# Graph convolution kernel: four buffers of marks and taken rows in the first and third convolution, and 28 gathered groups of the first turned into 20 bucketed ones

## The reference

```python
src, dst, norm = _gcn_norm(edge_index, n)          # with self loops, norm = deg^-1/2[src] * deg^-1/2[dst]
def _gcn_conv(x, src, dst, norm, W, b, n_nodes):
    h = x @ W
    msg = h[src] * norm[:, None]
    out = jax.ops.segment_sum(msg, dst, num_segments=n_nodes)
    return out + b
h = jnp.maximum(_layernorm(x, axis=-1), 0.0)
x = x + _L0_gnn_ref(h, edge_weight, edge_attr_3, edge_index, ...)
h = jnp.maximum(_layernorm(x, axis=-1), 0.0)
for W, b in ((W1, b1), (W2, b2), (W3, b3)):
    h = jax.nn.relu(_gcn_conv(h, src, dst, norm, W, b, n))
return x + h
```

## Time and profile before

| | |
|---|---|
| median of 3 runs | 4809.85 us (4805.98 to 4815.88) |
| the profiled execution: time, span | 4815.22 us, 4813.4 us |
| PE busy | 3897.2 us, 81% |
| DVE busy | 3588.3 us, 75% |
| POOL busy | 3497.7 us, 73% |
| ACT busy | 2682.7 us, 56% |
| indirect DMAs (line 760) | 3552, mean 977 ns |

### The profile page before, as it was taken

The page is one execution under the profiler, slowest core; times in us unless marked ns, Lnnn a source line. Parts: engine busy times, 40 slices in busy tenths (PEclk is TensorE's granted clock), DMA queues, the critical chain, the costliest instruction groups (busy, mean ns, idle before and its releaser), DMA issues.

```text
span 4813.4 us, 182574 instructions
## 1 busy us (share of the span) xinstructions
PE 3897.2 (81%) x69021; PEld 2928.7 (61%) x69022; DVE 3588.3 (75%) x8527; ACT 2682.7 (56%) x6468; POOL 3497.7 (73%) x3596
## 2 busy tenths in 40 slices
PE   4988888888888888847666666898999999777776
PEld 2655555555555555535555555688888887556564
DVE  8999999999999999878777777544444444666666
ACT  4555555555555555468777777455555555544443
POOL 6777777777777777547777777477777776577775
PEclk9999999999999999956555555899999999776766
DMA  3111111111112112333333333443434444445544
GB/s 100 41 40 40 40 40 40 40 40 40 40 40 40 40 40 40 41 69 99 92 85 91 92 92 84 125 116 114 122 114 117 120 115 119 132 145 147 146 146 119
DMA packets 493903, 401.86 MB, mean 83 GB/s; under 512 B 266471, under 2 KB 454796, under 8 KB 492481
## 3 DMA queue, kind: packets, MB, share of 16 engines
q10 hardware_dynamic: 150164, 212.59, 13.1%
q0 software_dynamic: 113664, 104.82, 11.7%
q1 hardware_dynamic: 229360, 74.44, 7.1%
HBM read 376.21 MB, written 15.29 MB: 81 GB/s over the span
## 4 chain that ended last, share of the span: by engine, by line
POOL 68%; issue 23%; DVE 3%; PE 3%; ACT 1%; DMA 1%; POOLq 1%; DVEq 0%; ACTq 0%; SPq 0%
POOL rows L760 68%; PE radial L2168 1%; PE radial L2028 0%; DMA rows<-table,idx 0%; PE radial L2181 0%; ACT accT L926 0%; PE sums L1903 0%; DVE scratch L1098 0%; DMA xn<-in_x 0%; DMA scratch<-places_d 0%; DMA table<-arena 0%; PE radial L1969 0%; DVE rows L1788 0%; PE radial L1982 0%; PE psX L2046 0%
## 5 line engine op out<-in xcount | busy, mean ns | idle before, releaser
L760 POOL DMA_INDIRECT rows<-table,idx x3552 | 3471.2, 977 | 1237.9 <-issue 1138.0
L2028 PE MATMUL radial<-arena,shared 128*32 128x96 bf16 (+1 forms) x32400 | 936.7, 266 | 193.2 <-DVE shared L1578 80.3
L1903 PEld LDWEIGHTS sums<-scratch,onehot 128*64 128x64 f32 x9408 | 796.2, 136 | 395.6 <-DVE scratch L1342 229.1
L1903 PE MATMUL sums<-scratch,onehot 128*64 128x264 f32 (+1 forms) x9408 | 924.9, 340 | 69.5 <-DVE scratch L1342 58.0
L2028 PEld LDWEIGHTS radial<-arena,shared 128*32 128x32 bf16 (+1 forms) x32400 | 706.5, 115 | 315.0 <-issue 99.0
L1325 DVE TENSOR_TENSOR scratch<-radial,shared 128x768 f32<-128x768 f32 x784 | 741.3, 946 | 0.0
L983 ACT CAST scratch<-radial 128x480 bf16<-128x480 f32 x860 | 476.3, 554 | 460.3 <-PE radial L2028 440.7
L1888 PE MATMUL radial<-shared 64*128 64x384 f32 x3136 | 639.7, 485 | 0.0
L826 ACT ACTIVATE dist<-iota,rel 128x64 f32<-128x64 f32 (+1 forms) x2304 | 601.8, 343 | 44.3 <-issue 23.3
L856 ACT COPY shared<-rows 128x192 f32<-128x192 f32 x196 | 88.9, 454 | 841.1 <-DMA rows<-table,idx 830.3
L1317 DVE TENSOR_TENSOR scratch<-radial,shared 128x512 f32<-128x512 f32 x784 | 533.6, 681 | 13.3 <-issue 13.3
(11 more groups left out here) (230 smaller groups left out, 5276.2 us busy)
## 6 DMA issues: line engine op xcount, KB each, us to landing
scratch<-places_d ACTq DMA_DIRECT2D x248, 800.0 KB
rows<-table,idx POOLq DMA_INDIRECT x3552
shared<-in_edge_weight SPq DMA_DIRECT2D x390, 128.0 KB
idx<-in_src SPq DMA_DIRECT2D x443, 4.0 KB
table<-arena SPq DMA_DIRECT2D x24, 256.0 KB, 2.5
table<-arena SPq DMA_DIRECT2D x2, 1176.0 KB, 10.6
accT<-in_edge_attr SPq DMA_DIRECT2D x2, 1152.0 KB
table<-arena SPq DMA_DIRECT2D x24, 96.0 KB, 2.0
```

What stands on the lines that cost most here:

```text
L760: (pool.indirect_dma_start(rows_3[:, r, j, :] if n in (1, 3) else rows[:, r, j, 0:WIDTH[n]], None, tables[n], bass.IndirectOffsetOnAxis(ap ...
L1903: last = nc.tensor.matmul(there, onehot[:, u % 2, 4 * h + t, 0:SW], taken_from, start=(h + q + part == 0), stop=(h == 1 and q == 1 and par ...
L2028: last = nc.tensor.matmul(d, from_src[n][:, h, i, t, :], table_of(n, s), start=True, stop=True, tile_position=(0, 32 * i))
```

## The change

The first convolution has 64 gathered groups where it had 92, and 96 bucketed ones where it had 76: its 8 iterations are all of 8 gathered groups and 12 bucketed ones (60 chunks), as in the third. The number of ranks is the same, 2 ahead, 12 in each of 7 iterations and 10 in the last. In the first and third convolution `from_src`, `to_dst` and `taken` have four buffers. In the body of chunk `k` ACT now makes the marks of `k + 3`, for `c` = 0, 2 and 3 (`NEAR`); DVE those of `k + 2` for `c` = 1 and 4 (`ODD`), in the third convolution for all, and the destinations of `k + 1`. The places of a group are loaded at other chunks. The second convolution is not touched.

```diff
-GATHERED = [NG, 92, 92, 64]
-LOOP = [(UNROLL, 0), (12, 10), (12, 10), (8, 12)]
-REST = [(UNROLL, 0), (8, 6), (8, 6), (8, 12)]
+GATHERED = [NG, 64, 92, 64]
+LOOP = [(UNROLL, 0), (8, 12), (12, 10), (8, 12)]
+REST = [(UNROLL, 0), (8, 12), (8, 6), (8, 12)]
...
+NEAR, ODD = (0, 2, 3), (1, 4)
+DEPTH = [0, 4, 2, 4]
+AHEAD_SRC = [0, 2, 1, 2]
+AHEAD_NEAR = 3
+AHEAD_DST = [0, 1, 0, 1]
...
@@ near_sources, on ACT
-                if not no_chunk(1, step, k - 2):
-                    act.wait_ge(bucket_taken, chunk_count(1, step, k, -2))
+                if not no_chunk(1, step, k - DEPTH[1]):
+                    act.wait_ge(bucket_taken, chunk_count(1, step, k, -DEPTH[1]))
...
@@ body, on ACT
-                        more = not (last and k == chunks_ - 1)
-                        if n == 1 and more and (k + 1) % NCK != NCK - 1:
-                            near_sources(step, k + 1)
+                        near = n == 1 and (k + AHEAD_NEAR) % NCK in NEAR and not (last and k + AHEAD_NEAR >= chunks_)
+                        if near:
+                            near_sources(step, k + AHEAD_NEAR)
...
-                        if n == 1 and c == 1 and not (last and k + NCK >= chunks_):
-                            load_places(n, step, v + 1)
-                        if n > 1 and c == NCK - 1 and not (last and k + 2 * NCK >= chunks_):
-                            load_places(n, step, v + 2)
+                        if k in ({max(4 * i + 5, i * NCK + NCK - 1) for i in range(chunks_ // NCK)} if n == 1 else
+                                 range(NCK - 1, chunks_, NCK)):
+                            if not (last and (v + (c == NCK - 1) + 1) * NCK >= chunks_):
+                                load_places(n, step, v + (c == NCK - 1) + 1)
...
@@ body, on DVE
-                        more = not (last and k == chunks_ - 1)
-                        if more and (n > 1 or (k + 1) % NCK == NCK - 1):
-                            mark_sources(n, step, k + 1)
-                        mark_destinations(n, step, k)
+                        if (n > 1 or (k + AHEAD_SRC[1]) % NCK in ODD) and not (last and k + AHEAD_SRC[n] >= chunks_):
+                            mark_sources(n, step, k + AHEAD_SRC[n])
+                        if not (last and k + AHEAD_DST[n] >= chunks_):
+                            mark_destinations(n, step, k + AHEAD_DST[n])
```

More of the change, by code:

```diff
@@ L99 @@
 NORM_HEAD = 12 * P
+assert all(LOOP[n][1] * NCK % DEPTH[n] == 0 and REST[n][1] * NCK % 2 == 0 for n in (1, 2, 3))
 assert PLAST * BJ == E - E0 - (NBG - 1) * BE and 4 * KB >= NB
@@ L107 @@
 assert RANKS % SLOTS == 0 and 4 * RANKS + 2 <= LOOP[1][1] * NCK and OWN_LAST == REST[1][1] - 2
-assert OWN_LAST <= RANKS_LAST and 3 * RANKS_LAST == REST[1][1] * NCK
+assert OWN_LAST <= RANKS_LAST and 3 * RANKS_LAST < REST[1][1] * NCK
 NORM0 = sqrt(4 * pi) / sqrt(2 * MUL)
@@ L974, in copy_bucket @@
                 act.wait_ge(bucket_taken, chunk_count(n, step, k))
-                if not no_chunk(n, step, k - 2):
-                    act.wait_ge(bucket_summed, chunk_count(n, step, k, -2))
+                if not no_chunk(n, step, k - DEPTH[n]):
+                    act.wait_ge(bucket_summed, chunk_count(n, step, k, -DEPTH[n]))
                 h = k % 2
@@ L982, in copy_bucket @@
                 else:
-                    nc.scalar.copy(taken[n][:, h, :, :], radial[0][:, h, 0:KC * F3].rearrange(
+                    nc.scalar.copy(taken[n][:, k % DEPTH[n], :, :], radial[0][:, h, 0:KC * F3].rearrange(
                         "p (t f) -> p t f", f=F3)).then_inc(bucket_copied, 1)
@@ L1009, in body @@
                                 copy_prefix(step, i)
-                        if n == 1 and more and (k + 1) % NCK != NCK - 1:
-                            mark_sources(step, k + 1)
+                        if near:
+                            mark_sources(step, k + AHEAD_NEAR)
                         copy_bucket(n, step, k)
@@ L1014, in body @@
                         for i, part in parts:
-                            if part == 1 and last:
+                            if part == 1 and last and i < RANKS_LAST:
                                 copy_prefix(step, i)
@@ L1018, in body @@
                                 store_places(step, i - 1, last)
-                        if n == 1 and c == 1 and not (last and k + NCK >= chunks_):
-                            load_places(n, step, v + 1)
-                        if n > 1 and c == NCK - 1 and not (last and k + 2 * NCK >= chunks_):
-                            load_places(n, step, v + 2)
-                    if last and n == 1:
-                        store_places(step, RANKS_LAST - 1, last)
+                        if k in ({max(4 * i + 5, i * NCK + NCK - 1) for i in range(chunks_ // NCK)} if n == 1 else
+                                 range(NCK - 1, chunks_, NCK)):
+                            if not (last and (v + (c == NCK - 1) + 1) * NCK >= chunks_):
+                                load_places(n, step, v + (c == NCK - 1) + 1)
                 if n == 1:
-                    near_sources(Step(act, 0, n), 0)
-                    mark_sources(Step(act, 0, n), 0)
+                    for k in range(AHEAD_NEAR):
+                        if k in NEAR:
+                            near_sources(Step(act, 0, n), k)
+                            mark_sources(Step(act, 0, n), k)
                 if n == 2:
@@ L1037, in first_places @@
                 load_places(n, Step(act, 0, n), 0)
-                if n == 2:
+                if n < 3:
                     load_places(n, Step(act, 0, n), 1)
@@ L1599, in mark_destinations @@
                     dve.wait_ge(dst_paired, pairs_made(n, step, v_))
-                if not no_chunk(n, step, k - 2):
-                    dve.wait_ge(bucket_summed, chunk_count(n, step, k, -2))
+                if not no_chunk(n, step, k - DEPTH[n]):
+                    dve.wait_ge(bucket_summed, chunk_count(n, step, k, -DEPTH[n]))
                 if n == 2:
@@ L1739, in body @@
                             ranking(step, k, last)
-                    if last and n == 1:
-                        keep_places(step, RANKS_LAST - 1, last)
                     if last:
@@ L1754, in conv @@
                     make_onehot(n, begin, 0, True)
-                if n > 1:
-                    mark_sources(n, Step(dve, 0, n), 0)
+                for k in range(AHEAD_SRC[n]):
+                    if n > 1 or k in ODD:
+                        mark_sources(n, Step(dve, 0, n), k)
+                for k in range(AHEAD_DST[n]):
+                    mark_destinations(n, Step(dve, 0, n), k)
                 sweep(dve, body, n)
@@ L2027, in take @@
                             d = radial[0][32 * i:32 * i + 32, h, t * F3:(t + 1) * F3]
-                        last = nc.tensor.matmul(d, from_src[n][:, h, i, t, :], table_of(n, s), start=True, stop=True,
+                        last = nc.tensor.matmul(d, from_src[n][:, k % DEPTH[n], i, t, :], table_of(n, s), start=True, stop=True,
                                                 tile_position=(0, 32 * i))
@@ L2141, in body @@
                         give(n, step, chunks_ - 1)
-                    if last and n == 1:
-                        place_values(step, RANKS_LAST - 1)
                 if n == 1:
```

34 lines of the change are left out of this document (17 added, 17 removed).

## The result

The changed kernel takes **4909.14 us** (median of 4 runs, 4907.34 to 4917.80) against 4807.91 us (4 runs, 4805.14 to 4815.88) before: ratio 1.0211, 95% interval 1.0194 to 1.0229, slower by some 101 us. The forecast was 4925 us and slower.

What follows compares the result with a forecast made beforehand. POOL's gathers bound the first convolution; afterwards DVE would where ranks run, ACT elsewhere. +16, +51 and +50 us make +117 us on 4815.2 us: 4932, 4927 on the median's scale, stated as 4925 us, range 4830 to 4985 us.

Steps and rivals of the forecast that it cites:

- The sum: First convolution: first iteration +16 us, six middle ones +51 us, last +50 us, together +117 us.
- POOL off the bound: First convolution: 287 us of gathers go, 512 remain taking 657 us against the stage's 962 us, so POOL no longer bounds.
- DVE's pace, 8.84 us a rank: First convolution, middle iterations, chunks with ranks: DVE bounds at 8.84 us per rank and four chunks, twelve taking 106 us.
- The added marks of sources: DVE in a rank's period: 1.6 marks of sources instead of one, adding 0.18 us.
- Chunks without ranks, 1.72 us each by ACT: Twelve chunks an iteration, 30 in the last: ACT bounds at 1.72 us each, 20.6 us and 51.6 us.
- The last iteration: First convolution's last iteration: 136.6 us against 87.0 us before, +50 us.
- The load right behind the store, 2 us: Third and fourth groups of each iteration: ACT waits for a store before the load, 2 us an iteration, bounds 0 and 6.
- The branch, 2 us: Branch back in the six middle iterations, now paid by whichever engine bounds: 2 us each, bounds 0 and 3 us.
- The third convolution, 0: Third convolution: POOL's gathers at 1.262 us each cover all of it, so it costs and gives nothing.
- clock: Rival, first convolution: a higher granted clock brings PE's table sooner, -28 us, 4897 us; inside the range, no separate chance.
- Short tails: Rival, first convolution: waits hidden, ACT 1.4 us a chunk, period 8.6 us; +34 us, 4845 us; no separate chance.
- Evened out: Rival, first convolution: four buffers make DVE's total count, -35 us, 4775 us, middle iteration under 122 us; chance 0.09.

Runs made afterwards that it cites:

- run 6: Changed kernel with one more 0.75 us product of two SBUF operands on DVE in each rank, result unused: 4977.45 us, ratio 1.0353.
- run 10: Changed kernel with ACT's marks one chunk ahead instead of three, and the third and fourth groups' loads of places one chunk later: 4889.35 us, ratio 1.0151.
- run 4: Changed kernel with ACT making four of five pairs of marks instead of three, four buffers kept: 4945.06 us, ratio 1.0292.
- run 5: Changed kernel with ACT making two of five pairs of marks instead of three, four buffers kept: 4902.90 us, ratio 1.0202.
- run 3: Changed kernel with the chunks without ranks spread out between ranks, same work in another order: 4834.44 us, ratio 1.0046.
- run 2: Kernel before with only the third convolution's part of the change: 4808.46 us, ratio 1.0007.
- run 12: Changed kernel with ranks spread out, ACT's marks one chunk ahead and the loads one chunk later: 4798.94 us, ratio 0.9977.
- run 7: Kernel before with one more DVE product in each rank, both operands in SBUF: 4858.00 us, ratio 1.0102.
- run 8: Kernel before with one more 0.75 us DVE instruction in each rank, one operand in PSUM: 4840.74 us, ratio 1.0045.

## Why the prediction was right

The sum was +117 us for the stage; the starts of ranks say +105. Who bounds next, and where, came out as forecast; that the sum came so near is in part luck, as the terms show:

- **POOL off the bound**: right. 512 gathers with 365 us of waiting for sums. (By the earlier trace rows all engines were busy for 65% to 75% of the stage before, not 63% to 75%; nothing hangs on it.)
- **DVE's pace, 8.84 us a rank**: right in kind (run 6: every microsecond more in a rank counts) and nearly in size. Without the waits for store and load it is 8.7 us (run 10); the change shows 9.0 because of them. The added marks of sources were priced too high, since work beside a rank's chain shows only in part (runs 4 to 6). In the first and the last iteration, taken at 8.4 and 7.8 us, it was (2211.51 - 2119.91) / 11 = 8.33 and (3094.79 - 3025.06) / 9 = 7.75 us with these waits among them, and 7.9 and 7.5 us in run 10: here values that were too high met a loss that was counted elsewhere.
- **Chunks without ranks, 1.72 us each by ACT**: right in kind (runs 3, 4), a little too dear. The wait for a load, which the prediction had counted, belongs to the pace: by run 5 fewer marks on ACT don't shorten these chunks, and by run 10 it goes when ACT marks only one chunk ahead. Timeline of ACT of the changed kernel, last iteration, behind its last rank: three loads of places, a mark that waits for one, and the last copy:
```profile
3098.23 0.45 ACTq L949 DMA_DIRECT2D scratch<-places_d  x1
...
3106.03 0.40 ACTq L949 DMA_DIRECT2D scratch<-places_d  x1
...
3110.72 0.83 ACT L966 ACTIVATE shared<-scratch,line 128x640 bf16<-128x640 bf16 x1 [1.04 <-DMA scratch<-places_d]
...
3114.18 0.40 ACTq L949 DMA_DIRECT2D scratch<-places_d  x1
...
3144.92 0.56 ACT L988 CAST scratch<-radial 128x480 bf16<-128x480 f32 x1 [0.53 <-PE radial L2035]
```
  From the load at the end of chunk 29 to the end of chunk 59's copy are 47.25 us, 1.58 us a chunk; the wait for a load was 0.6 to 1.2 us, not 1.65. The last iteration, 136.6 us in the forecast, was 127.1: 4 us of it by this, and 4 more because the last rank, taken as a full period of 7.8 us ahead of the chunks without ranks, lay beside them (its start at 3094.79 us is only 3.4 us ahead of the end of chunk 29). In a middle iteration the last rank, twelve such chunks and the branch were 31.4 us in the forecast and 32.8 in the trace.
- **The load right behind the store, 2 us**: the mis-sized term, too low, though within its bounds of 0 and 6 us. The store cost 2.72 us of ACT before the copy of a prefix, the load behind it 3.02 us. Run 10, which takes both away, gives 4.5 to 4.8 us in a middle iteration ((3000.24 - 2369.47) / 5 = 126.15 against 130.9): 3.0 us among the ranks, where this term was, and 1.5 us in the gap. The prediction said "More buffers don't shorten it"; that the look-ahead that came with them could make it longer, because ACT's marks three ahead ask for a group's places two chunks earlier than marks one ahead, it priced only as "perhaps 2 us more".
- **The branch, 2 us**: too low, and counted once too often. Only five of the six middle iterations end in a branch back. From their last rank to the next iteration's first they take 32.2 to 33.2 us, 32.8 on average; the sixth, with the same chunks, takes 29.3 us (to 3025.06 us), and in run 10 it is 31.3 and 28.1 us. So a branch back costs 3.2 to 3.4 us here, if the straight code that follows the sixth isn't itself what is quicker. ACT's first marks behind it show 3.9 to 4.1 us of idle time.
- **The third convolution, 0**: right (run 2).

So of the 12 us between sum and trace the first and the last iteration made 3 and 9.5 us. The middle ones came out at 130.6 forecast and 130.8 measured because DVE's pace, a little too dear, made up for the store's and the branch's terms, both too low. Of the rivals, *clock* didn't come about: the granted clock was 0.59, 0.58 before. *Short tails* needs 1.4 us a chunk, and it was 1.58. *Evened out* fell: a middle iteration was not under 122 us. Yet what it named is what runs 3 and 12 do by order instead of buffers: four buffers let engines run past one another for two or three chunks, not for twelve. That is argued from their depth. The PSUM tile of taken rows and the places kept two buffers in all of these kernels, so no run shows what more buffers everywhere would carry. The Trainium skill (Perfetto Trace Analysis, Optimization Strategy) says that regimes with different busiest engines may gain by being interleaved; run 3 agrees, with four fifths of the loss given back.

## What to carry to other kernels

When work is taken off the engine that bounds, ask what the next one does in each stretch and not in total: here DVE was busy for 74% of the stage, and yet set the pace wherever it had a rank, and stood idle for most of the time where it had none (from 2478.0 to 2502.4 us it was busy for 8.6 us). Keep the mix of work even down to single chunks, by the order in which it is written; here four buffers didn't do it for a block of twelve chunks. And marks made further ahead ask for their inputs as much earlier: where the load isn't moved with them, as here, the look-ahead can cost more than it gives. Keep a load off the queue position right behind a store that it has to wait for. When an edit of several parts shows no effect, look for parts that cancel: here one of +0.6% and one of -0.8% stood behind it.

## What the runs showed of the hardware that was not expected

**DVE holds up POOL's indirect DMAs.** Most gathers take 0.94 us, a few more. In run 7 the timeline of POOL has
```profile
2172.02 0.94 POOL L760 DMA_INDIRECT rows<-table,idx  x1 [0.30 <-issue]
2173.27 2.25 POOL L760 DMA_INDIRECT rows<-table,idx  x1 [0.30 <-issue]
2175.82 0.94 POOL L760 DMA_INDIRECT rows<-table,idx  x1 [0.30 <-issue]
```
and that of DVE
```profile
2173.29 0.74 DVE L1522 TENSOR_TENSOR dist<-arena 128x1144 bf16<-128x1144 bf16 x1
2173.95 0.74 DVE L1524 TENSOR_TENSOR arena<-arena 128x1144 bf16<-128x1144 bf16 x1
2174.73 0.46 DVE L1527 TENSOR_TENSOR arena<-arena 128x572 bf16<-128x572 bf16 x1
2175.22 0.31 DVE L1529 TENSOR_TENSOR arena<-arena 128x286 bf16<-128x286 bf16 x1
2175.56 0.45 DVE L1531 TENSOR_REDUCE arena<-arena 128x11 f32<-128x286 bf16 x1
```
The long gather ends at 2175.52 us, with the last of four instructions that read two tensors of SBUF one right behind the other (2175.53); 83 of 96 gathers over 1.05 us in that run end within 0.06 us of the same instruction's end. What such gathers took over 0.95 us adds up to 19.4 us in the kernel before, 64.3 us in run 7 and 22.7 us in run 8, where the added instruction reads PSUM. The difference of 45 us is what run 7 lost in the stage. The Trainium skill (SBUF — State Buffer, Who interferes with whom) says that a VectorE instruction with two SBUF inputs contends with a GpSimd instruction that reads SBUF, and that the loser is blocked for the whole instruction. The rows agree, and show that a chain of such instructions can hold on: 1.3 us for one gather, which had started 0.02 us ahead of the first of them. The Trainium skill infers in the same section that such products don't hold up the descriptors of a DMA; the indirect DMAs here were held up, and the measurement decides.

**The places' load and the store before it.** The load of 800 KB let its reader go 4.2 to 4.9 us behind its issue, the store of a rank's places 2.6 us or more behind its own, as in the rows shown at run 10.
